# Two layers of attention and feed-forward on one core: the front of the first batch in the setup, stacks from two queues, gates broadcast by halves, expert weights loaded one per batch

## The chip, the core and the metric

The kernel runs on one core of one Trainium2 chip. The engines are TensorE (PE, with its weight loads PEld), VectorE (DVE), ScalarE (ACT), GpSimd (POOL) and SyncE (SP), which here only issues transfers; in the kernel before it issues all of them. The metric is the device time of one execution in microseconds.

## The reference, cut to what matters

x is 8 batches of 512 tokens by 128 channels. Each of two layers has an attention part and a feed-forward part, both modulated by a conditioning vector per batch:

```python
mod = (_silu(L0_c) @ L0_wmod).reshape(L0_c.shape[0], 6, 1, -1)
sa, ca, ga, sb, cb, gb = (mod[:, 0], mod[:, 1], mod[:, 2], mod[:, 3], mod[:, 4], mod[:, 5])
ga = (2 * (ga >= 0) - 1) * jnp.maximum(jnp.abs(ga), 0.25)
gb = (2 * (gb >= 0) - 1) * jnp.maximum(jnp.abs(gb), 0.25)
h = _layernorm(x, axis=-1) * (1 + ca) + sa
x = x + ga * _L0_attn_ref(h, ...)      # 16 heads of 8, causal
h = _layernorm(x, axis=-1) * (1 + cb) + sb
x = x + gb * _L0_ffn_ref(h, ...)       # 8 experts of 176, two per token, and a shared one
# layer 1: the same frame; attention with ALiBi slopes and no mask, then a spiking feed-forward
```

```python
scores = jnp.einsum('bhqk,bhsk->bhqs', q, k) / jnp.sqrt(jnp.float32(dk))
scores = jnp.where(causal_mask, jnp.float32(-1000000000.0), scores)
weights = jax.nn.softmax(scores, axis=-1)
ctx = jnp.einsum('bhqs,bhsk->bhqk', weights, v)
return concat @ Wo + bo
```

## The kernel before

The program has five parts, one after the other: the setup, the attention of layer 0, its experts, the attention of layer 1, its spiking feed-forward. Each part is a block in which every engine has its own instruction list; a block ends when all engines are through their lists. The change is in the setup and in the first batches of the attention of layer 0.

**Setup** (`setup_phase`, from L107). SP issues the loads: cT, x of batch 0, wmod (the modulation weights, 768 KB), columns (projection weights and biases), rows, then x of batches 1 to 7 (1.75 MB), and the constant rows of the stacks. TensorE makes the gates of both layers (`setup_ps<-wmod,c_silu`, L171), eight modulations (`setup_ps<-c_silu,wmod`, L178), and the output bias. VectorE makes the layer norm statistics of batch 0, the SiLU, the gates, mods (shift and scale per channel) and scales the q weights. GpSimd clears tiles and normalises batch 0 (xn).

**The front of a batch** (helpers `front_*`, L299 to L405). VectorE makes the statistics, GpSimd 1/std and xn, TensorE transposes xn (L337), ScalarE reads it with shift and scale into hT (L355), TensorE projects q, k (L349) and v (L346), ScalarE reads q and k twice (bf16 in L363, f32 in L364) and v into VP (L369). q and k in f32 are split into three bf16 parts each by `front_split` (L374): subtract, round, subtract. SP stacks the parts into QP and KP with six transfers each (`front_stack`, L391). A matmul over such a stack gives the score of f32 q and k.

**The attention** (`attention_phase`, L408). Heads are worked in groups of four, four groups a batch, 32 groups G in all. Time goes by beats, six beats a group, 24 a batch in layer 0, and every engine's list is written by one loop over the beats from -11 to the end. Beat 0 is that of group 0's first key score. Max scores run 11 beats ahead (`max_score`, L569 and L580): queries on the partitions, VectorE reduces them (L829, L833), GpSimd makes the negative maximum in two bf16 parts (`shifts`, L915 to L918), TensorE transposes it (`max_T`, L550), ScalarE copies it (at_nrow, L742), and SP sends it with two transfers into two rows of QP (`send_rows`, L1007). Then come the key scores (`key_score`, L606), ScalarE's exponentials (L757), GpSimd's clearing above the diagonal (L946), and the values (`values`, L654) into Ob, which ScalarE copies once a group (Oev, L785). Max scores use two double banks of PSUM, key scores and fronts share three banks in turn.

SP's list is in order: a transfer waits behind all that are written before it. Per batch b it has the Q stack of b + 1, rows of group 4b + 1, the K stack of b + 1, the denominators and results of batch b - 1 gathered (den, ctxN, L241), rows of 4b + 2, the reciprocals spread through DRAM (rdram, denB, L257), rows of 4b + 3 and 4b + 4. The context of batch b - 1 is multiplied by denB on VectorE (L268), projected by TensorE with weights that GpSimd has multiplied by the gate (`finish_weights`), and added to x.

Fronts of batch n are written into batch n - 2's beats: ln at 14, q at 17, k at 20, and v at 6 of batch n - 1. For batch 1 that is beats -10, -7 and -4. Batch 0's front stands ahead of the beats.

Of the kernel before, what the change touches and what calls it, by code (L numbers as in the profile page):

```python
# [13 lines left out]
F32 = mybir.dt.float32  # L14
# [7 lines left out]
P = 128  # L22
# [83 lines left out]
def setup_phase(nc, dram, sb):  # L106

    x, ident = sb["x"], sb["ident"]
    with ExitStack() as ctx:
# [12 lines left out]
        s = semaphores(nc, ctx, "su", "c x0 bop wmod load zero ident tanh sil mm chain")  # L122
# [5 lines left out]
        def _(sp):  # L128
# [4 lines left out]
            sp.dma_start(sb["columns"][:], dram["columns"]).then_inc(s["load"], 16)  # L133
            sp.dma_start(sb["rows"][:], dram["rows"].partition_broadcast(P)).then_inc(s["load"], 16)
            sp.dma_start(x[:, SEQ:].rearrange("p (m d) -> p m d", d=D),
                         dram["x"][1:].rearrange("b (t p) d -> p (b t) d", p=P)).then_inc(sb["x_rest"], 16)
# [3 lines left out]
            sp.wait_ge(s["load"], 32)  # L140
            sp.wait_ge(s["chain"], 5)
            sp.dma_start(sb["gates_dram"], sb["gate_rows"][:]).then_inc(sb["gates_sent"], 16)

        @block.gpsimd
        def _(g):
            g.memset(ident[:], 0.0).then_inc(s["zero"], 1)
            g.memset(sb["mhalf"][:], -0.5)
            g.memset(sb["ones"][:], 1.0)
            g.memset(sb["VP"][:], 0.0).then_inc(s["zero"], 1)
# [3 lines left out]
            g.wait_ge(s["zero"], 2)  # L153
            g.memset(sb["VP"][:, :, :, :, DENS:DENS + 1], 1.0)
            front_powers(g, sb, front, 0)
            front_normalise(g, sb, front, 0)

        @block.scalar
# [5 lines left out]
        def _(t):  # L164
            t.wait_ge(s["sil"], 1)
            t.wait_ge(s["wmod"], 16)

# [7 lines left out]
            for layer in range(2):  # L175
                for i, ch in enumerate((CH_SA, CH_CA, CH_SB, CH_CB)):
                    k = layer * 4 + i
                    last = t.matmul(ps[:, 1, k * NBATCH:(k + 1) * NBATCH], wmod[:, layer, ch * D:(ch + 1) * D],  # L178
                                    sil[:, layer, :], start=True, stop=True)
            last.then_inc(s["mm"], 1)  # L180
            t.wait_ge(s["load"], 32)
# [11 lines left out]
        def _(v):  # L193
            v.wait_ge(s["x0"], 16)
            front_stats(v, sb, front, 0)
# [211 lines left out]
def attention_phase(nc, dram, sb, layer):  # L407
# [5 lines left out]
    with ExitStack() as ctx:  # L413
# [64 lines left out]
        def fills(beat):  # L478
# [5 lines left out]
            for name, when, lead in (("ln", LN_AT, 2), ("q", Q_AT, 2), ("k", K_AT, 2), ("v", V_AT, 1)):  # L484
                if at == when and 1 <= n + lead <= last_b:
                    out.append((name, n + lead))
# [1422 lines left out]
```

## Time and profile before

| | us |
|---|---|
| median of 3 runs | 1073.48 |
| lowest and highest | 1072.3 and 1075.61 |
| profiled execution | 1077.53 |
| its span on the core | 1075.8 |
| TensorE busy | 951.1 |
| VectorE busy | 784.7 |
| ScalarE busy | 755.6 |
| GpSimd busy | 539.2 |

The span is what the profiler sees on the engines, the profiled execution's own time is a little more. A busy time is that of instructions; a matmul row gives its modelled end, so a busy TensorE is not one at its peak. A line such as L349 can be a helper's and then stands for many places; the tile names and the time say which one it is. An x2 behind an f32 matmul's row means two records for each. "SPq" rows are issues of transfers by SP, with the time that the issuing took, not the transfer.

### The profile page before, as it was taken

How to read it: one execution, taken by the hardware profiler on the slowest of the kernel's cores; microseconds unless marked ns; L12 is line 12 of the kernel's file. 1: busy time of each engine (PE TensorE's matmuls, PEld its weight loads, DVE VectorE, ACT ScalarE, POOL GpSimd, SP SyncE). 2: the span in 40 equal slices, each digit the busy share in tenths (PEclk: the TensorE clock that was granted, in tenths of full speed). 3: DMA queues.
4: the chain of work that ended last, by engine and by line, in shares of the span. 5: the costliest groups of instructions: out<-in, count | busy, mean ns of one | idle time of the engine just before them, and what ended most of it. 6: DMA issues, size and time to landing. Idle time of an engine off the chain costs nothing. (4 is left out here: it accounts for less than half of the span.)

```text
span 1075.8 us, 23037 instructions
## 1 busy us (share of the span) xinstructions
PE 951.1 (88%) x8688; PEld 519.9 (48%) x8688; DVE 784.7 (73%) x1321; ACT 755.6 (70%) x1380; POOL 539.2 (50%) x751
## 2 busy tenths in 40 slices
PE   5688898889898999999999889989899998899896
PEld 3233343334344888888888623333333333333564
DVE  2567777778793766776766589888898988896465
ACT  2367777777776666666666459888888888888663
POOL 4446655675553011101130557786867778665344
PEclk9589999999999999999999979999999999999999
DMA  6432212211301533321343320203112020200011
GB/s 187 155 127 76 57 41 78 72 42 54 84 13 53 130 108 110 91 85 49 102 109 99 93 78 19 74 12 83 31 54 62 24 73 13 82 2 25 23 30 50
DMA packets 61246, 73.91 MB, mean 69 GB/s; under 512 B 14088, under 2 KB 43400, under 8 KB 60624
## 3 DMA queue, kind: packets, MB, share of 16 engines
q1 hardware_dynamic: 61136, 72.44, 24.0%
q8 instruction: 69, 1.13, 0.5%
q14 instruction: 41, 0.34, 0.1%
HBM read 39.24 MB, written 2.77 MB: 39 GB/s over the span
## 5 line engine op out<-in xcount | busy, mean ns | idle before, releaser
L757 ACT ACTIVATE at_E<-at_Sb 128x512 f32<-128x512 f32 x832 | 446.4, 598 | 94.6 <-PE at_Sb L606 88.9
L826 DVE TENSOR_REDUCE at_mx<-at_Mb 128x2 f32<-128x1024 f32 x256 | 297.2, 1217 | 39.8 <-PE at_Mb L569 38.7
L654 PE MATMUL at_Ob<-at_E,VP 128*32 128x256 f32 (+2 forms) x2816 | 215.0, 379 | 13.0 <-ACT Oev L785 7.3
L606 PE MATMUL at_Sb<-QP,KP 64*128 64x512 bf16 (+3 forms) x1024 | 202.6, 346 | 13.4 <-ACT full_k L364 3.6
L569 PE MATMUL at_Mb<-KP,QP 62*128 62x512 bf16 (+3 forms) x1024 | 181.5, 361 | 31.1 <-DVE at_mx L826 28.2
L935 POOL TENSOR_TENSOR at_E<-at_E,at_factor 128x512 f32<-128x512 f32 x128 | 162.4, 1272 | 79.7 <-ACT at_E L757 69.7
L829 DVE TENSOR_REDUCE at_mx<-at_Mb 128x2 f32<-128x768 f32 (+1 forms) x128 | 138.2, 1087 | 72.3 <-PE at_Mb L569 71.1
L946 POOL TENSOR_SCALAR_AFFINE_SELECT at_E<-at_E 128x512 f32<-128x512 f32 x128 | 82.7, 659 | 83.2 <-ACT at_E L757 83.2
L569 PEld LDWEIGHTS at_Mb<-KP,QP 62*128 62x128 bf16 x1024 | 55.0, 97 | 125.9 <-DVE at_mx L826 73.4
L654 PEld LDWEIGHTS at_Ob<-at_E,VP 128*32 128x32 f32 x2816 | 57.0, 108 | 115.2 <-issue 86.0
L606 PEld LDWEIGHTS at_Sb<-QP,KP 64*128 64x128 bf16 x1024 | 74.8, 96 | 74.1 <-ACT at_E L757 34.9
L1355 DVE TENSOR_TENSOR ex_hh<-ex_R,ex_th 128x512 f32<-128x512 f32 x88 | 66.0, 751 | 57.9 <-ACT ex_th L1299 57.2
L1299 ACT ACTIVATE ex_th<-ex_z 128x512 f32<-128x512 f32 x88 | 55.6, 632 | 67.7 <-DVE ex_z L1345 66.4
L1345 DVE SCALAR_TENSOR_TENSOR ex_z<-ex_Ab,columns,ex_up 128x512 f32<-128x512 f32 x104 | 77.7, 748 | 30.9 <-ACT ex_up L1284 27.2
L1457 PEld LDWEIGHTS ex_Yb<-ex_w,ex_hh 128*128 128x128 f32 x704 | 91.3, 191 | 13.6 <-DVE ex_hh L1355 7.1
L1457 PE MATMUL ex_Yb<-ex_w,ex_hh 128*128 128x128 f32 x704 | 93.5, 276 | 3.7 <-DVE ex_hh L1355 3.7
L1284 ACT ACTIVATE ex_up<-ex_Bb,columns 128x512 f32<-128x512 f32 x104 | 70.9, 682 | 16.5 <-PE ex_Bb L1441 11.3
L1065 POOL TENSOR_TENSOR ex_rstd<-ex_ve,mhalf 128x4 f32<-128x4 f32 x8 | 8.2, 1020 | 146.9 <-DVE ex_ve L1059 146.9
L833 DVE TENSOR_REDUCE at_mx<-at_Mb 128x4 f32<-128x1024 f32 x64 | 59.9, 953 | 5.1 <-PE at_Mb L569 4.3
L654 PE MATMUL at_Ob<-at_E,at_VD 128*32 128x128 f32 (+1 forms) x1024 | 60.5, 332 | 0.0
L1439 PE MATMUL ex_Ab<-ex_h_hi,ex_w_hi 128*128 128x512 f32 x104 | 50.2, 483 | 2.4 <-PEq L413 1.3
L785 ACT ACTIVATE Oev<-at_Ob 128x512 f32<-128x512 f32 x64 | 38.9, 607 | 5.9 <-PE at_Ob L654 5.9
(185 smaller groups left out, 1428.3 us busy)
## 6 DMA issues: line engine op xcount, KB each, us to landing
QP<-q SPq DMA_DIRECT2D x96, 128.0 KB, 2.4
KP<-k SPq DMA_DIRECT2D x96, 128.0 KB, 2.4
ex_R<-rw_dram SPq DMA_DIRECT2D x32, 256.0 KB, 4.2
ctxN<-Oev SPq DMA_DIRECT2D x16, 256.0 KB, 2.9
denB<-rdram SPq DMA_DIRECT2D x64, 64.0 KB
ex_R<-rw_dram SPq DMA_DIRECT2D x16, 224.0 KB, 4.5
ex_R<-rw_dram SPq DMA_DIRECT2D x16, 192.0 KB, 3.6
ex_R<-rw_dram SPq DMA_DIRECT2D x16, 160.0 KB, 3.4
```

Source lines behind the costliest of these rows:

```text
L569: return pe.matmul(out[:, c, at:at + width], QP[p0:p0 + ROWS_M, b % 2, hp, qt * P:(qt + 1) * P], KP[p0:p0 + ROWS_M, b % 2, hp, 0:width], s ...
L606: return pe.matmul(out[:, at:at + SEQ - q0], KP[p0:p0 + ROWS_H, b % 2, 2 * g + a, kt * P:(kt + 1) * P], QP[p0:p0 + ROWS_H, b % 2, 2 * g + ...
L654: last = pe.matmul(Ob[VW * i:VW * (i + 1), 0, q0:q1], weights_of(b, G, kt, i, q0), moving, start=(kt == 0 and q0 == 0), stop=False, skip_g ...
L757: nc.scalar.activation(dst, src, ACT.Exp).then_inc(s["s_read"], 1)
L826: v.tensor_reduce(mx[:, G % 2, :, t % 2, t // 2], src, AX.X, ALU.max).then_inc(s["m_read"], 1)
L829: v.tensor_reduce(mx[:, G % 2, :, t % 2, qt], src[:, :, 0:(qt + 1) * P], AX.X, ALU.max)\
L935: p.tensor_tensor(blocks, blocks, factor[:, GROUP * g:GROUP * (g + 1), :], ALU.mult)\
L946: last = p.affine_select(out=blocks, in_=blocks, compare_op=ALU.is_ge, fill=0.0, base=0, pattern=[[0, GROUP], [1, P]], channel_multiplier=-1)
L1284: nc.scalar.activation(up3[:, q, :], Bb[:, q, :], ACT.Identity, bias=b3[:, j:j + 1]).then_inc(s["u3"], 1)
L1345: v.scalar_tensor_tensor(z[:, q, :], Ab[:, q, :], b1[:, j:j + 1], up3[:, q, :], ALU.add, ALU.mult).then_inc(s["z"], 1)
L1355: v.tensor_tensor(hh[:, r % 2, :], R[:, r % RING, :], th[:, r % 2, :], ALU.mult)\
L1457: last = pe.matmul(Yb[:, 0, t * P:(t + 1) * P], hidden[:, t * P:(t + 1) * P], w2[:, j, :], start=(j == 0 and t == 0), stop=(j == N - 1), s ...
```

## The change

In the setup, the SiLU goes ahead of the statistics. The two modulations that layer 0's attention needs come first, then the gates, then the whole front of batch 0: transposes, hT, q, k, v, in four PSUM banks of its own (`setup_front`). GpSimd splits q, VectorE splits k. SP issues Q's stack and ScalarE K's, both within the setup. The other six modulations and the output bias come behind. x of batch 1 is loaded on its own.

In the attention of layer 0, the front of batch 0 is gone from the lists, the front of batch 1 moves from beats -10, -7 and -4 to -2, 1 and 4, and its statistics from ahead of the beats to behind beat -8's reduction. x of batches 2 to 7 is loaded behind group 0's rows. The gates (`gates`, broadcast from DRAM to 128 partitions, 2 MB) come in two halves of 1 MB: layer 0's in batch 0 behind group 2's rows, layer 1's in batch 2 behind group 10's rows. Of w1, w3 and w2 (832 KB each) one is loaded in each of batches 1, 2 and 3. The lists of layer 1 keep their order; it only waits for its half of the gates.

```diff
 setup, SP
-            sp.dma_start(x[:, SEQ:].rearrange("p (m d) -> p m d", d=D),
-                         dram["x"][1:].rearrange("b (t p) d -> p (b t) d", p=P)).then_inc(sb["x_rest"], 16)
             front_rows(sp, dram, sb, 0, 0, front["const"])
             for name in ("maskq", "maskk"):
                 sp.dma_start(sb[name][:], dram[name]).then_inc(front["const"], 16)
+            sp.dma_start(x[:, SEQ:2 * SEQ].rearrange("p (t d) -> p t d", t=TILES),
+                         dram["x"][1].rearrange("(t p) d -> p t d", p=P)).then_inc(sb["x1"], 16)
+            sp.dma_start(sb["rows"][:], dram["rows"].partition_broadcast(P)).then_inc(s["load"], 16)
+            front_stack(sp, sb, front, 0, 0, 2)
 setup, GpSimd
+            g.wait_ge(front["s_read"], 2)
+            front_split(g, sb, front, "q", 0)
 setup, ScalarE
+            a.wait_ge(s["mods"], 1)
+            a.wait_ge(front["s_fill"], 1)
+            front_hT(nc, sb, front, 0, 0, fb[:, 0, :])
+            a.wait_ge(s["scaled"], 1)
+            for i, which in enumerate("qk"):
+                a.wait_ge(front["s_fill"], 2 + i)
+                front_qk(nc, sb, front, 0, which, fb[:, 1 + i, :])
+            a.wait_ge(s["vp"], 1)
+            a.wait_ge(front["s_fill"], 4)
+            front_v(nc, sb, front, 0, fb[:, 3, :])
+            front_stack(a, sb, front, 1, 0, 3)
 setup, TensorE
+            modulation(0, 0)
+            modulation(0, 1).then_inc(s["mm"], 1)
...
+            front_transpose(t, sb, front, 0, fb[:, 0, :])
+            t.wait_ge(s["scaled"], 1)
+            t.wait_ge(front["s_read"], 1)
+            for i, which in enumerate("qkv"):
+                front_project(t, sb, front, 0, which, fb[:, 1 + i, :])
+            for layer, i in ((0, 2), (0, 3), (1, 0), (1, 1), (1, 2), (1, 3)):
+                last = modulation(layer, i)
 setup, VectorE
+            v.tensor_tensor(full[:], full[:], parts["k0"][:], ALU.subtract).then_inc(front["r"], 1)
+            v.wait_ge(front["r"], 2)
+            v.wait_ge(front["p1"], 1)
+            v.tensor_copy(parts["k1"][:], full[:]).then_inc(front["p1"], 1)
+            v.wait_ge(front["p1"], 2)
+            v.wait_ge(front["p2"], 1)
+            v.tensor_tensor(parts["k2"][:], full[:], parts["k1"][:], ALU.subtract).then_inc(front["p2"], 1)
 attention, beats
+        EARLY = {-2: "ln", 1: "q", 4: "k"} if causal else {}
 attention, VectorE
+                if causal and beat == -8:
+                    v.wait_ge(sb["x1"], 16)
+                    front_stats(v, sb, s, 1)
+                    front_aggregate(v, sb, s, 1)
 attention, GpSimd
+                if causal and beat == -7:
+                    front_powers(p, sb, s, 1)
+                    normalise(1)
+                if causal and beat in EARLY and beat > 0:
+                    split(EARLY[beat], 1)
 attention, SP
-                stack(0, 0)
-                stack(0, 1)
-                sp.wait_ge(sb["gates_sent"], 16)
-                sp.dma_start(sb["gates"][:], sb["gates_dram"].partition_broadcast(P)).then_inc(sb["gates_ready"], 16)
+            send_rows(0)
+                sp.dma_start(sb["x"][:, 2 * SEQ:].rearrange("p (m d) -> p m d", d=D),
+                             dram["x"][2:].rearrange("b (t p) d -> p (b t) d", p=P)).then_inc(sb["x_rest"], 16)
+                if b == 0 and causal:
+                    send_rows(1)
+                    stack(1, 0)
+                    stack(1, 1)
+                elif b < last_b:
                     stack(b + 1, 0)
+                    send_rows(GROUPS * b + 1)
                     stack(b + 1, 1)
-                if b == 0 and causal:
-                    for dst, src in ((sb["w_raw"]["w1"], "w1"), (sb["w_raw"]["w3"], "w3"), (sb["w2"], "w2")):
-                        sp.dma_start(dst[:], dram[src]).then_inc(sb["experts_loaded"], 16)
+                if 1 <= b <= 3 and causal:
+                    dst, src = ((sb["w_raw"]["w1"], "w1"), (sb["w_raw"]["w3"], "w3"), (sb["w2"], "w2"))[b - 1]
+                    sp.dma_start(dst[:], dram[src]).then_inc(sb["experts_loaded"], 16)
+                if b == 0 and causal:
+                    sp.wait_ge(sb["gates_sent"], 16)
+                    sp.dma_start(sb["gates"][:, :, 0:2 * P], ...).then_inc(sb["gates_ready"], 16)
+                if b == 2 and causal:
+                    sp.dma_start(sb["gates"][:, :, 2 * P:4 * P], ...).then_inc(sb["gates_late"], 16)
```

What this does to the lists is seen at two places. First TensorE, from the end of the setup to the first key scores. at_Mb are max scores, at_Sb from `ident,xn` the transposes of batch 1, from `hT,columns` its q or k, from `idb,at_nmx` the transposed maximum, from `QP,KP` key scores. Before:

```order
L337 MATMUL at_Sb<-ident,xn 128x128 x4
...
L569 MATMUL at_Mb<-KP,QP 128x256 x4
L349 MATMUL at_Sb<-hT,columns 128x512
L589 MATMUL at_Mb<-maskk,maskq 128x256 x2
...
L550 MATMUL at_Sb<-idb,at_nmx 32x128
L349 MATMUL at_Sb<-hT,columns 128x512
L580 MATMUL at_Mb<-maskk,maskq 128x128 x2
...
L606 MATMUL at_Sb<-QP,KP 128x512 x2
```

And now:

```order
L605 MATMUL at_Sb<-idb,at_nmx 32x128
L635 MATMUL at_Mb<-maskk,maskq 128x128 x2
...
L387 MATMUL at_Sb<-ident,xn 128x128 x4
L644 MATMUL at_Mb<-maskk,maskq 128x2x128 x2
...
L661 MATMUL at_Sb<-QP,KP 128x512 x2
L399 MATMUL at_Sb<-hT,columns 128x512
L635 MATMUL at_Mb<-maskk,maskq 128x128 x2
...
L661 MATMUL at_Sb<-QP,KP 128x256 x2
L399 MATMUL at_Sb<-hT,columns 128x512
```

Batch 1's transposes now stand behind the transposed maximum of group 0, and its two projections behind key scores of beats 1 and 4. Second SP, from the first stack on. Before:

```order
L403 DMA QP<-q 16x8x512 x6
L403 DMA KP<-k 16x8x512 x6
...
L1019 DMA gates<-gates_dram 128x4096
L1007 DMA QP<-at_nrow 2x8x128 x2
L403 DMA QP<-q 16x8x512 x6
L1007 DMA QP<-at_nrow 2x8x128 x2
L403 DMA KP<-k 16x8x512 x6
L1031 DMA w_raw<-in_w 128x1664 x2
L1031 DMA ex_w<-in_w 128x1664
L1007 DMA QP<-at_nrow 2x8x128 x6
```

And now, from the first row transfers on:

```order
L1055 DMA QP<-at_nrow 2x8x128 x2
L1065 DMA x<-in_x 128x24x128
L1055 DMA QP<-at_nrow 2x8x128 x2
L453 DMA QP<-q 16x8x512 x6
L453 DMA KP<-k 16x8x512 x6
L1055 DMA QP<-at_nrow 2x8x128 x2
L1091 DMA gates<-gates_dram 128x8x256
L1055 DMA QP<-at_nrow 2x8x128 x4
L453 DMA QP<-q 16x8x512 x6
L1055 DMA QP<-at_nrow 2x8x128 x2
L453 DMA KP<-k 16x8x512 x6
L1082 DMA w_raw<-in_w 128x1664
```

The three weight matrices no longer stand together ahead of group 2's rows; x of batches 2 to 7 stands ahead of group 1's rows, half of the gates ahead of group 3's, and the first weight matrix behind the K stack of batch 2.

## Rows read from the trace of the kernel before

**Rows 1.** page section 1, busy time, share of the span and instructions:
```profile
PE 951.1 (88%) x8688; PEld 519.9 (48%) x8688; DVE 784.7 (73%) x1321; ACT 755.6 (70%) x1380; POOL 539.2 (50%) x751
```

**Rows 2.** windows: stretch, length, busy (x instructions) per engine, PEclk, DMA share, GB/s:
```profile
30.00:40.00 10.00, 8.06 (x42) 2.82 (x42) 6.82 (x7) 2.04 (x3) 1.18 (x3) 0.50 0.74 271
...
60.00:70.00 10.00, 6.28 (x58) 2.05 (x62) 5.29 (x12) 4.31 (x10) 5.09 (x11) 0.73 0.58 238
```

**Rows 3.** timeline, setup: start, us, engine, line, op, out<-in, [idle before, releaser]:
```profile
6.55 1.87 PE L171 MATMUL setup_ps<-wmod,c_silu 128*8 128x128 f32 x8 [6.55 <-DMA wmod<-in_wmod]
...
6.94 1.74 POOL L328 TENSOR_SCALAR xn<-x,nmean,rstd 128x128 f32<-128x128 f32 x4
...
8.35 3.58 PE L178 MATMUL setup_ps<-c_silu,wmod 128*128 128x8 f32 x16
...
14.86 0.42 DVE L232 COPY bopB<-setup_ps 128x256 f32<-128x256 f32 x1 [1.31 <-PE setup_ps L188]
...
16.01 1.08 PE L337 MATMUL at_Sb<-ident,xn 128*128 128x128 f32 x4 [1.19 <-PEq L109]
...
21.37 3.83 SPq L403 DMA_DIRECT2D QP<-q  x6
...
23.49 1.07 ACT L369 ACTIVATE VP<-at_Sb 128x512 f32<-128x512 f32 x1 [0.44 <-PE at_Sb L346]
...
25.25 3.85 SPq L403 DMA_DIRECT2D KP<-k  x6
...
31.05 0.29 PE L580 MATMUL at_Mb<-maskk,maskq 64*128 64x128 bf16 x2 [7.60 <-DMA KP<-k]
```

**Rows 4.** timeline, statistics of one batch and the beats before the first exponential:
```profile
4.16 0.87 DVE L303 BATCH_NORM_STATS2 st<-x 128x6 f32<-128x128 f32 x4 [4.16 <-DMA x<-in_x]
...
5.80 1.02 POOL L321 TENSOR_TENSOR rstd<-ve,mhalf 128x4 f32<-128x4 f32 x1 [0.60 <-DVE ve L315]
...
31.80 4.09 DVE L829 TENSOR_REDUCE at_mx<-at_Mb 128x2 f32<-128x1024 f32 x4 [13.81 <-PE at_Mb L569]
...
35.84 2.07 PE L349 MATMUL at_Sb<-hT,columns 128*128 128x512 f32 x2
...
43.18 0.27 PE L550 MATMUL at_Sb<-idb,at_nmx 128*32 128x128 bf16 x1 [3.22 <-POOL at_nmx L918]
...
48.32 0.63 PE L606 MATMUL at_Sb<-QP,KP 64*128 64x512 bf16 x2
```

**Rows 5.** timeline, the row transfers of groups 1 and 2:
```profile
52.59 1.15 SPq L1007 DMA_DIRECT2D QP<-at_nrow  x2
...
54.86 0.10 PEld L606 LDWEIGHTS at_Sb<-QP,KP 64*128 64x128 bf16 x2 [0.17 <-DMA QP<-at_nrow]
...
57.64 1.09 SPq L1031 DMA_DIRECT2D w_raw<-in_w  x2
...
60.17 23.98 SPq L1007 DMA_DIRECT2D QP<-at_nrow  x6
...
66.84 0.61 PE L606 MATMUL at_Sb<-QP,KP 64*128 64x512 bf16 x2 [3.28 <-DMA QP<-at_nrow]
```

**Rows 6.** timeline, ScalarE's reading of each group's result, groups 0, 1, 4, 5:
```profile
61.09 0.60 ACT L785 ACTIVATE Oev<-at_Ob 128x512 f32<-128x512 f32 x1
...
74.86 0.61 ACT L785 ACTIVATE Oev<-at_Ob 128x512 f32<-128x512 f32 x1
...
102.56 0.60 ACT L785 ACTIVATE Oev<-at_Ob 128x512 f32<-128x512 f32 x1
...
110.86 0.61 ACT L785 ACTIVATE Oev<-at_Ob 128x512 f32<-128x512 f32 x1
```

**Rows 7.** timeline, one projection; rows of group 6 and their first reader:
```profile
76.18 1.12 PE L349 MATMUL at_Sb<-hT,columns 128*128 128x512 f32 x2
...
101.64 1.19 SPq L1007 DMA_DIRECT2D QP<-at_nrow  x2
...
104.91 0.38 PE L606 MATMUL at_Sb<-QP,KP 64*128 64x512 bf16 x2
```

More of the change, by code:

```diff
@@ L173, in _ @@
             last.then_inc(s["mm"], 1)
[L175 to L179, printed above, removed]
+            t.wait_ge(s["ident"], 1)
+            front_transpose(t, sb, front, 0, fb[:, 0, :])
[5 more added lines that the diff above has]
+                last = modulation(layer, i)
             last.then_inc(s["mm"], 1)
-            t.wait_ge(s["load"], 32)
             for layer in range(2):
@@ L193, in _, with modulated, scale @@
         def _(v):
-            v.wait_ge(s["x0"], 16)
-            front_stats(v, sb, front, 0)
-            front_aggregate(v, sb, front, 0)
+            def modulated(layer, i):
+                k = layer * 4 + i
+                return v.tensor_scalar(sb["mods"][:, layer, i, :], ps[:, 1, k * NBATCH:(k + 1) * NBATCH],
+                                       float(i % 2), None, ALU.add)
+            def scale(layer):
+                for name, width in (("wqkv", D), ("bqk", 1)):
+                    w = sb[f"{name}{layer}"][:, 0:width]
+                    last = v.tensor_scalar(w, w, float(DK) ** -0.5, None, ALU.mult)
+                return last
             v.wait_ge(s["tanh"], 1)
@@ L201, in _ @@
             v.tensor_scalar(sil[:], sil2[:], 0.5, None, ALU.mult).then_inc(s["sil"], 1)
+            v.wait_ge(s["x0"], 16)
+            front_stats(v, sb, front, 0)
+            front_aggregate(v, sb, front, 0)
             v.wait_ge(s["mm"], 1)
+            modulated(0, 0)
+            modulated(0, 1).then_inc(s["mods"], 1)
+            v.wait_ge(s["columns"], 16)
+            scale(0).then_inc(s["scaled"], 1)
+            v.wait_ge(s["mm"], 2)
             src = ps[0:NBATCH, 0, :]
@@ L483, in fills @@
             n, at = divmod(beat, BPB)
+            if beat in EARLY:
+                out.append((EARLY[beat], 1))
             for name, when, lead in (("ln", LN_AT, 2), ("q", Q_AT, 2), ("k", K_AT, 2), ("v", V_AT, 1)):
-                if at == when and 1 <= n + lead <= last_b:
+                if at == when and (FIRST if lead == 2 else 1) <= n + lead <= last_b:
                     out.append((name, n + lead))
@@ L1739, in build @@
                 sb[n] = sb[whole][:, parts[n]:parts[after]]
[L1740 removed]
+        for n in ("x1", "x_rest", "gates_late", "gates_sent", "gates_ready", "stored", "apart"):
             sb[n] = ctx.enter_context(nc.semaphore(n))
```

90 lines of the change are left out of this document (39 added, 51 removed).

## The prediction

> **What bounds the kernel now.** I read the page first: TensorE is busy for 88% of the span and no other engine for more than 73% [rows 1]. That is an average over stages. The change touches the start and the first batches, so the windows of ten microseconds come next: in 30 to 40 the granted clock is 0.50, half of the 2.4 GHz level, and in 60 to 70 it is 0.73 with TensorE busy for 6.28 of 10 us [rows 2]. These are the two places where time can be had, and the timeline says why.
>
> At the start TensorE waits 7.60 us for the K stack: the twelve stack transfers leave one queue, Q's six from 21.37 and K's six from 25.25, 3.85 us for six, and the first max score starts at 31.05 [rows 3]. From there to the first key score at 48.32 it is 17.27 us, for 11 beats. In them stand both projections of batch 1, of which the first takes 2.07 us at the low clock, and a wait of 3.22 us for GpSimd, which splits batch 1's q before it makes group 0's shifts [rows 4].
>
> At 63.6 a second hole opens: group 2's row transfer is issued at 60.17, behind three weight matrices of 832 KB issued from 57.64 on, and its reader starts at 66.84 after a wait of 3.28 us [rows 5]. The price is read from ScalarE's result copies: groups 0 to 1 lie 13.77 us apart, the undisturbed groups 4 to 5 lie 8.30 apart, so the hole and the slow clock behind it cost 5.5 us [rows 6].
>
> **Part 1, front of batch 0 in the setup.** The SiLU goes ahead of the statistics on VectorE, which moves nothing: TensorE's first matmul waits for wmod until 6.55 either way. Then come two modulations (3.58 us for eight, 0.45 each: 0.9) and the four gate matmuls (1.87), until 9.3. xn is ready at 8.68, so the four transposes start at 9.3 where they started at 16.01 [rows 3]: 6.7 us earlier. What follows up to the reading of v is the same chain on the same engines, so v is read by 24.56 - 6.7 = 17.9, Q's stack is issued from 14.7 to 18.5, and K's, now on ScalarE's queue behind that reading, from 17.9 to 21.7. Before, K's data was usable 1.95 us after the last issue (29.10 to 31.05), so now at 23.7. The setup itself must also end: v's matmuls end at about 16.8, six modulations add 2.7, and from there to the next block is what lay between 11.93 and 16.01, 4.1 us: 23.6 [rows 3]. I take 23.8 for the first max score, 7.2 earlier. SP's issues of constants no longer stand behind 1.75 MB of x, so I see nothing of them on this path.
>
> No row shows ScalarE issuing a transfer. The nearest row is SP's, 0.64 us each; at twice that K's stack would come 3.8 us later, at nothing it would still wait for its third part and for the end of the setup. So 0 to 3.8 us against, and I take 0.
>
> VectorE makes k's parts instead of GpSimd. Its three operations lie within the time in which ScalarE issues K's first three transfers (1.9 us from 17.9), and k is read before v, so by 16.8 (23.49 - 6.7). I count it at nothing; on GpSimd it would have stood behind q's parts.
>
> What the second queue is worth is small: on SP alone K's issues would start at 18.5 and not at 17.9, so 0.6 us. The Trainium skill speaks against more (DMA: Bandwidth & Descriptors, Issuing engines are not separate DMA queues): queues share the same 16 DMA engines, and a second one saves only the sequencer's time. By that rule, the sum holds as it stands, since I count no faster transfer; whoever counts on two parallel streams would put 3.8 us more into it.
>
> **Part 2, the beats before the first key score.** The statistics of batch 1 now stand on VectorE after four reductions: 4.09 us for four, and 1.64 us from the statistics' start to GpSimd's power (4.16 to 5.80) [rows 4]. So: 23.8 + 0.75 until VectorE starts + 4.09 + 1.64 = 30.3; power and normalisation end 2.88 us later (5.80 to 8.68) [rows 3, 4] at 33.2; group 0's shifts are queued behind them on GpSimd, and with the transpose and the copy on ScalarE I give them 1.6 us, to 34.8. A row transfer needs 2.3 us from issue to reader (52.59 to 54.86) [rows 5]: 37.1. By VectorE alone: ten reductions at 1.02 and the statistics give 36.4, and 0.7 of TensorE: the same 37.1. I take 37.2 for the first key score against 48.32: 11.1 us earlier. TensorE no longer stops for long between 9.3 and there, so I expect the full clock in it; VectorE sets the pace, and I count nothing for it.
>
> **Part 3, q and k of batch 1 in beats 1 and 4.** They are no longer in the beats before. Now they stand among key scores: 1.12 us each at full clock [rows 7], 2.24, with ScalarE's four readings ahead of exponentials. Ends: 0, where TensorE waits for VectorE anyway, and 4.1, both at the low clock [rows 4]. I take 2.5.
>
> **Part 4, weights spread, gates halved, x last.** The hole in batch 0 goes: 5.5 us. What is late next are the other transfers ahead of row transfers. A row transfer has 3.3 us from issue to need (101.64 to 104.91) [rows 7] and uses 2.3, so its slack is 1.0 us. Ahead of one there now are 1.5 MB of x (group 1's rows, issued about five us later), one weight matrix in each of batches 1 to 3, before the gathering of the denominators, which VectorE waits for in order, and half of the gates in batches 0 and 2, the latter before the denominators' way through DRAM. The 2.5 MB took from 57.64 to about 65 [rows 5], so 0.34 MB a microsecond: 832 KB need 2.5 us, of which all but the last part passes before the rows of group 6 are issued 3 us later. Low end 0. High end: each is wholly in front of its reader, 4.4 + 2.9 + 3 x 2.5 + 2.9 less 1.0 of slack each, some 12 us. I take 2.5: 0.5 for each matrix and 1 for the late gates, near the low end, because the queue's issues keep them apart.
>
> **The sum.** 11.1 - 2.5 + 5.5 - 2.5 = 11.6 us. The profiled execution took 1077.53 us (span 1075.8), so 1065.9; it lies 4 us above the median 1073.48, and on the median's scale the forecast is 1062.
>
> **Rivals.**
> (a) The end of the setup moves by less: ScalarE's issues are slow, or the constants come late. For it speaks that TensorE's order in the setup is now one chain through four engines; against it, that each step has a row. Price 3 to 5 us: 1066.
> (b) Batch 1 comes late. Its k is read in beat 4, split by GpSimd behind three diagonal operations, and stacked on SP; A beat is 1.4 us (8.30 / 6) [rows 6]: k is projected by 5 x 1.4 + 1.1 = 8.1 after the first key score, reading and split with their queues are some 5, the last issues and the landing 3, so 16; TensorE asks for it in beat 13, at 13 x 1.4 + 2.5 = 20.7. A margin of 4 to 5, estimated from these rows. If the splits slip a group, TensorE waits 4 us with a lower clock behind it: 1066 to 1068.
> (c) Each large transfer stops its reader for about its whole length, but the clock holds: 12 in place of 2.5, gain 2: 1071.
> (d) Slower than before: the same waits, each drawn out as the one in the trace was, where 3.28 us of waiting cost 5.5, a factor of 1.7, since the clock fell behind it [rows 2, 5, 6]. The place is the key score that opens groups 1, 6, 10, 14 and the context of batch 1. 12 x 1.7 = 20 in place of 2.5: 1062 + 17.5 = 1079. It decides from 8.3 us of pure waiting on. Against it: the weights were three in a row, and no two large transfers now stand together.
> (e) More is gained: the projections of part 3 hide, and no new wait shows: 5 us more, 1057.
>
> **How the numbers follow.** Forecast, 1058 to 1066: 0.60. (a) 0.10 and (b) 0.08, both faster; (c) 0.08, of which 0.05 within 0.3%; (d) 0.05, of which 0.01 within; (e) 0.09. 0.3% is 3.2 us, about what a measurement of this kernel can tell from no change. Faster 0.60 + 0.10 + 0.08 + 0.03 + 0.09 = 0.90, same 0.06, slower 0.04. The range 1055.5 to 1069 leaves out (c), (d) and a little of (e).
>
> **What would show it.** In the profile after: transposes at about 9.3, K's six issues on ScalarE's queue from about 17.9, the first max score at about 23.8 with a granted clock of 1.00 before and behind it, the first key score at 37.2, groups 0 and 1 read about 8.7 us apart, q and k of batch 1 between key scores at 1.12 us. Wrong would be: a wait of TensorE for a row transfer in groups 1, 6, 10 or 14, of VectorE for den or denB in batches 1 to 3, or of TensorE for the stacks at beat 13, of more than 1 us each. The forecast falls if the first key score stands later than 41, or if batches 1 to 3 together take over 5 us longer than before.

## The result and the profile after

The changed kernel took 1065.92 us (median of 5 runs, 1064.44 to 1066.16), the kernel before 1075.61 beside it (5 runs, 1072.3 to 1078.66): a ratio of 0.9908 [0.9881, 0.9935], 9.7 us less. Run again with the experiments it gave 0.9906 [0.9872, 0.994] and 0.9934 [0.9914, 0.9955]. The profiled execution took 1066.16 us, its span is 1064.4 where it was 1075.8.

Section 1 of the page after, engines busy in us, answers to [rows 1]: the work is the same, the span is shorter.

```profile
PE 945.7 (89%) x8688; PEld 517.6 (49%) x8688; DVE 788.3 (74%) x1324; ACT 754.2 (71%) x1380; POOL 537.5 (50%) x748
```

Two windows of it, with the columns of [rows 2]:

```profile
30.00:40.00 10.00, 6.18 (x43) 2.51 (x45) 9.20 (x19) 0.78 (x2) 3.32 (x8) 0.50 0.01 3
...
60.00:70.00 10.00, 9.14 (x103) 3.68 (x99) 6.71 (x8) 8.21 (x17) 5.75 (x12) 1.00 0.09 29
```

In 30 to 40 the granted clock is still 0.50, against the forecast, but VectorE is busy for 9.20 of 10 us where it had 6.82: it sets the pace there. In 60 to 70 TensorE works for 9.14 us at the full clock (1.00); the hole is gone.

The timeline of the front, answering to [rows 3] and [rows 4]:

```profile
8.88 0.99 PE L184 MATMUL setup_ps<-c_silu,wmod 128*128 128x8 f32 x4 [8.88 <-DMA wmod<-in_wmod]
...
11.61 1.12 PE L387 MATMUL setup_front<-ident,xn 128*128 128x128 f32 x4
...
17.19 4.04 SPq L453 DMA_DIRECT2D QP<-q  x6
...
18.84 4.09 ACTq L453 DMA_DIRECT2D KP<-k  x6
...
23.30 0.42 DVE L282 COPY bopB<-setup_ps 128x256 f32<-128x256 f32 x1 [0.80 <-PE setup_ps L214]
...
27.05 0.29 PE L635 MATMUL at_Mb<-maskk,maskq 64*128 64x128 bf16 x2 [3.79 <-DMA KP<-k]
...
37.17 0.27 PE L605 MATMUL at_Sb<-idb,at_nmx 128*32 128x128 bf16 x1 [1.32 <-POOL at_nmx L966]
...
40.43 0.63 PE L661 MATMUL at_Sb<-QP,KP 64*128 64x512 bf16 x2
...
42.23 1.13 PE L399 MATMUL at_Sb<-hT,columns 128*128 128x512 f32 x2
...
46.29 1.13 PE L399 MATMUL at_Sb<-hT,columns 128*128 128x512 f32 x2
```

Here wmod landed at 8.88, where it landed at 6.55 before, and everything behind it is late by as much. The last two rows are q and k of batch 1, now among key scores. The same kernel profiled again (a0 below) had wmod at 6.21, and is the better copy to compare:

```profile
6.21 1.00 PE L184 MATMUL setup_ps<-c_silu,wmod 128*128 128x8 f32 x4 [6.21 <-DMA wmod<-in_wmod]
...
9.01 1.09 PE L387 MATMUL setup_front<-ident,xn 128*128 128x128 f32 x4
...
14.56 4.03 SPq L453 DMA_DIRECT2D QP<-q  x6
...
16.21 4.01 ACTq L453 DMA_DIRECT2D KP<-k  x6
...
24.01 0.29 PE L635 MATMUL at_Mb<-maskk,maskq 64*128 64x128 bf16 x2 [2.87 <-DMA KP<-k]
```

A table by stage says where the time went. Its borders are starts of rows: the first max score, the first key score, and ScalarE's result copies (Oev, line 836, [rows 6]) of groups 0, 1, 14, 31 (end of layer 0's attention), 32 (the first of layer 1's attention, with layer 0's experts ahead of it) and 63 (its last). All in us, one profiled execution each.

| stage | before | after | a0 | a1 | e1 | e2 | e9 | e8 |
|---|---|---|---|---|---|---|---|---|
| to first max score | 31.05 | 27.05 | 24.01 | 23.96 | 24.37 | 24.77 | 24.18 | 22.57 |
| to first key score | 17.27 | 13.38 | 13.35 | 13.36 | 13.36 | 13.36 | 13.37 | 13.37 |
| to group 0 | 12.77 | 15.43 | 15.64 | 15.72 | 16.72 | 15.39 | 15.65 | 15.50 |
| groups 0 to 1 | 13.77 | 8.17 | 8.15 | 8.16 | 16.28 | 8.16 | 8.15 | 8.18 |
| groups 1 to 14 | 121.55 | 126.07 | 126.62 | 124.00 | 121.94 | 122.73 | 124.55 | 122.82 |
| groups 14 to 31 | 145.37 | 145.45 | 145.39 | 145.37 | 145.36 | 145.37 | 144.67 | 145.48 |
| groups 31 to 32 | 308.50 | 308.73 | 308.81 | 310.05 | 308.72 | 308.73 | 308.55 | 308.87 |
| groups 32 to 63 | 352.01 | 346.64 | 348.89 | 350.55 | 349.08 | 350.75 | 345.22 | 345.28 |

a0 and a1 are the changed kernel again, the e's are experiments. Down to group 14 the change is worth 6.3 us in the first profile, 8.6 in a0 and 11.2 in a1. The row below that one no edit of the change touches, and it hardly moves. The last row holds layer 1's attention, which the change leaves as it is but for waiting for its half of the gates, and yet three profiles of one kernel lie 3.9 us apart in it; e9 is about that.

What is new between groups 1 and 14 stands in ScalarE's rows of the profile after, beside the queue's:

```profile
87.91 0.60 SPq L1082 DMA_DIRECT2D w_raw<-in_w  x1
88.56 0.61 SPq L291 DMA_DIRECT2D den<-Oev  x1
89.21 0.58 SPq L292 DMA_DIRECT2D ctxN<-Oev  x1
...
94.31 0.60 ACT L836 ACTIVATE Oev<-at_Ob 128x512 f32<-128x512 f32 x1 [1.33 <-DMA ctxN<-Oev]
...
132.42 0.60 ACT L836 ACTIVATE Oev<-at_Ob 128x512 f32<-128x512 f32 x1 [2.89 <-DMA ctxN<-Oev]
...
171.47 0.60 ACT L836 ACTIVATE Oev<-at_Ob 128x512 f32<-128x512 f32 x1 [1.14 <-DMA ctxN<-Oev]
```

The copy of groups 4, 8 and 12 overwrites Oev, which the gathering of the batch before (ctxN) must first have read, and that gathering is issued 1.3 us behind a weight matrix. Before, these copies waited for no transfer [rows 6]. The waits view of the stretch 80 to 325 (what waited, for whom: us in total, times, longest) sums it and shows VectorE's, which I had priced instead:

```profile
ACT Oev L836 <- DMA ctxN<-Oev: 5.4, 3, 2.9
...
DVE rden L299 <- DMA den<-Oev: 1.4, 1, 1.4
```

### The profile page after: what moved, and what is told of

The parts are those of the page before. It is cut to its first block and busy times, and to the rows that moved or that the text cites. A ratio compares the mean times of both kernels' runs of the same rounds, so it can differ in the third digit from the quotient of the medians.

```text
span 1064.4 us, 23048 instructions
## 1 busy us (share of the span) xinstructions
PE 945.7 (89%) x8688; PEld 517.6 (49%) x8688; DVE 788.3 (74%) x1324; ACT 754.2 (71%) x1380; POOL 537.5 (50%) x748
## 3 DMA queue, kind: packets, MB, share of 16 engines
q8 instruction: 69, 1.13, 0.4%
## 5 line engine op out<-in xcount | busy, mean ns | idle before, releaser
L709 PE MATMUL at_Ob<-at_E,VP 128*32 128x256 f32 (+2 forms) x2816 | 213.8, 377 | 16.5 <-ACT Oev L836 10.2
L624 PE MATMUL at_Mb<-KP,QP 62*128 62x512 bf16 (+3 forms) x1024 | 181.5, 360 | 23.6 <-DVE at_mx L872 20.3
L1342 ACT ACTIVATE ex_up<-ex_Bb,columns 128x512 f32<-128x512 f32 x104 | 70.9, 682 | 16.6 <-PE ex_Bb L1499 11.6
L836 ACT ACTIVATE Oev<-at_Ob 128x512 f32<-128x512 f32 x64 | 38.9, 608 | 11.2 <-PE at_Ob L709 5.9
```

The lines of the kernel that those rows point to most:

```text
L624: return pe.matmul(out[:, c, at:at + width], QP[p0:p0 + ROWS_M, b % 2, hp, qt * P:(qt + 1) * P], KP[p0:p0 + ROWS_M, b % 2, hp, 0:width], s ...
L709: last = pe.matmul(Ob[VW * i:VW * (i + 1), 0, q0:q1], weights_of(b, G, kt, i, q0), moving, start=(kt == 0 and q0 == 0), stop=False, skip_g ...
L1342: nc.scalar.activation(up3[:, q, :], Bb[:, q, :], ACT.Identity, bias=b3[:, j:j + 1]).then_inc(s["u3"], 1)
```

## The experiments

The theory after the result: the front gives 11, q and k of batch 1 cost little, one weight matrix per batch removes the 5.5 us hole and brings back some of it as ScalarE's waits for ctxN. The rivals: the weights never mattered; the front is set by the constants' order, by the number of queues, or by who makes k's parts. Runs of the kernel before on the same chip stand beside each.

**a0, the changed kernel again**, with 15 runs of the kernel before.

> The changed kernel itself, as the reference for the others on the same chip. The profiled one had its first max score at 27.05, its first key score at 40.43, the result of group 1 read at 64.03, of group 12 at 171.47 and of group 31 at 335.55. Theory A (the gain lies in layer 0 alone: 10.8 us by group 1, of which 4.5 are given back in batches 1 to 3; the rest of the 11.4 between the two profiled spans is layer 1 waiting for den and denB by chance): these five come within 0.3 us again and the time is 6 to 10 us below before. Rival B (layer 1 gains from the change as well, as its order of transfers differs): layer 1 again takes 5 us less than in the kernel before.

Measured: 1066.12 (1062.6 to 1069.82, 5 runs) against 1076.3 (1070.72 to 1080.31, 15 runs), 0.9906 [0.9872, 0.994]. In layer 0 its table column differs from the first profile by 3.0 us ahead of the first max score, where wmod landed 2.7 earlier, and by less than 0.6 in every row behind it. Neither theory came whole. The five runs lie 7.2 us apart, not 0.3. Layer 1's attention took 3.1 us less than in the one profile of the kernel before (A: nothing, B: 5), in a1 1.5 less, and the experiments that leave layer 1 alone range from 349.1 to 353.4 us there, around the 352.0 of before. So no gain of the change in layer 1 is shown.

**e1, the weights together again**: the three transfers back in one batch, at the same place.

```diff
-                if 1 <= b <= 3 and causal:
-                    dst, src = ((sb["w_raw"]["w1"], "w1"), ...)[b - 1]
-                    sp.dma_start(dst[:], dram[src]).then_inc(sb["experts_loaded"], 16)
+                if b == 0 and causal:
+                    for dst, src in ((sb["w_raw"]["w1"], "w1"), ...):
+                        sp.dma_start(dst[:], dram[src]).then_inc(sb["experts_loaded"], 16)
```

> The three weight matrices go back behind the K stack of batch 1, together; all else as in the changed kernel. Theory A: spreading them traded one hole for three waits (ScalarE's reading of groups 4, 8 and 12 waits for ctxN, which is queued behind a matrix). So here group 2's key score waits again some 3 us and groups 0 to 1 or 1 to 2 lie 4 to 6 us further apart, while the intervals before groups 4, 8 and 12 shrink by 2.0, 2.0 and 1.2 us: group 31 within 1 us of the changed kernel. Rival B (the prediction): the matrices cost 0.5 us each where they are now, so together they are 4 us slower.

Measured: 1071.23 (1067.43 to 1075.82, 10 runs), 0.9962 [0.9938, 0.9985], 5.1 us above a0. Its timeline, the queue's rows and the reader's:

```profile
53.34 1.10 SPq L1082 DMA_DIRECT2D w_raw<-in_w  x2
54.48 1.21 SPq L1082 DMA_DIRECT2D ex_w<-in_w  x1
55.73 1.14 SPq L1055 DMA_DIRECT2D QP<-at_nrow  x2
...
62.52 0.61 PE L661 MATMUL at_Sb<-QP,KP 64*128 64x512 bf16 x2 [5.92 <-DMA QP<-at_nrow]
```

A row transfer issued right behind three matrices reached its reader 6.8 us after its issue (55.73 to 62.52), where one alone needs 2.3 [rows 5]. Up to group 1 it takes 9.2 us longer than in a0, groups 1 to 14 are 4.7 shorter since the ctxN waits are gone; net 4.5 in layer 0, and 5.1 in the medians, with rival B's 4 nearer than theory A's 1. So spreading the weights is worth about half of the whole change, and the theory that they don't matter has fallen.

**e2, each weight matrix behind the last rows of its batch.**

```diff
+                send_rows(GROUPS * b + 3)
+                if 1 <= b <= 3 and causal:
+                    ...the same three lines, taken from ahead of the gathering
```

> Each matrix is issued behind the rows of the batch's fourth group, where SP then has nothing to issue for some 10 us, and no longer ahead of den and ctxN. Theory A: no wait of ScalarE for ctxN is left, groups 4, 8 and 12 are read 7.7 to 8 us behind their predecessors, group 31 comes 4.5 to 5.2 us earlier (330.8). Rival B: the waits for ctxN are not due to the matrix, and group 31 moves by less than 1.5.

Measured: no copy of Oev waits for ctxN in layer 0, and groups 1 to 14 take 122.73 (a0 126.62, a1 124.00). The median is 1065.06 (1064.35 to 1066.4, 4 runs), 1.1 below a0's, which is less than the runs differ by. The queue's and ScalarE's rows of e2, the same gathering and copy as above:

```profile
85.54 0.61 SPq L291 DMA_DIRECT2D den<-Oev  x1
86.19 0.58 SPq L292 DMA_DIRECT2D ctxN<-Oev  x1
...
90.59 0.60 ACT L836 ACTIVATE Oev<-at_Ob 128x512 f32<-128x512 f32 x1
```

So the mechanism is shown by the trace: with the matrix out of the way, the copy starts with no wait. Its price is 1.3 to 3.9 us in groups 1 to 14 (against a1 and a0), less than the 4.5 to 5.2 of theory A; by the medians alone it would not be shown. 1.2 us over before remain between groups 1 and 14, all of it between groups 1 and 4; which edit they belong to was not tried.

**e3, the constants issued once wmod has landed**: SP waits for wmod ahead of the spare rows and masks.

```diff
+            sp.wait_ge(s["wmod"], 16)
             front_rows(sp, dram, sb, 0, 0, front["const"])
```

> SP waits for wmod to land before it issues the constant rows, masks, x of batch 1 and rows. Theory A: wmod landed at 8.88 and not at 6.55 because four transfers of constants share the engines with it; without them TensorE starts at about 6.6, and the chain up to the stacks moves 2.2 us ahead: first max score at 25, group 31 2 us earlier. Rival B: the constants then come as late as the stacks, or wmod is late for another reason: first max score at 27 or later.

Measured: the first wmod matmul at 6.35 and the first max score at 24.47, as in a0 (6.21, 24.01); 1068.49 (1064.54 to 1070.32, 5 runs), 0.9922 [0.9891, 0.9952]. The edit shows nothing by itself, since the lateness did not come again without it either. But small transfers alone do not hold wmod back: in nine of ten further profiles of kernels that issue them as the changed one does, wmod was usable at 6.2 to 6.4, in one at 6.8 (e2), without any wait. The 8.88 of the first profile came in that one alone. What made it late is open.

**e4, the second half of the spare rows behind send_rows(0).**

```diff
-            if causal:
-                front_rows(sp, dram, sb, layer, 1, s["const2"])
...
+                front_rows(sp, dram, sb, layer, 1, s["const2"])
```

> The four transfers of constant rows for the second half of the stacks are issued behind group 0's rows and not at the start of the attention. In the changed kernel's second run SP issued Q's first part at 14.56, ScalarE issued K's last one by 20.22, and the first max score came at 24.01, 3.8 us later, with the transfer engines full. Theory A: the stacks are bound by the transfer engines, and these four (512 KB) run beside K's last parts: without them K lands 0.5 to 1.5 us earlier, 8 to 9 us behind Q's first issue. Rival B: the lag belongs to the second queue or to the end of the setup; 9.4 us as before.

Measured in one run: first max score at 23.91 with wmod at 6.20, first key score at 37.26, 1068.12 us. No effect, and the run could have had none: in a0 SP issues these four from 21.87 on, and from 22 to 23 ScalarE's queue (q10), with K's parts, is the only one that moves bytes.

```profile
q10 hardware_dynamic: 214, 0.19, 99.9%
```

So they never ran beside the stacks, and e4 does not test whether the transfer engines limit these.

**e5, both stacks on SP's queue.**

```diff
             front_stack(sp, sb, front, 0, 0, 2)
+            front_stack(sp, sb, front, 1, 0, 3)
...
-            front_stack(a, sb, front, 1, 0, 3)
```

> K's stack is issued by SP behind Q's, in the setup, and by no other queue. Theory A (bound by the transfer engines): the two stacks take 9.5 to 9.9 us from Q's first issue to the first max score, as on one queue in the kernel before (21.37 to 31.05, 9.68), against 9.45 with two; the second queue is worth less than 0.5 us. Rival B: the second queue hides K's issues, 3.8 us; then the first max score comes 2 us or more later than with two.

Measured in one run: 1068.8 us. Its timeline:

```profile
14.55 4.04 SPq L453 DMA_DIRECT2D QP<-q  x6
...
18.63 3.83 SPq L453 DMA_DIRECT2D KP<-k  x6
...
24.40 0.29 PE L635 MATMUL at_Mb<-maskk,maskq 64*128 64x128 bf16 x2 [3.27 <-DMA KP<-k]
```

On one queue K's last issue ends at 22.46 and the data is there 1.94 us later; on two it ends at 20.22 and the data comes 3.79 later (a0). From Q's first issue to the first max score it takes 9.85 us on one queue, and 8.94 to 9.86 with a mean of 9.54 in ten profiles with two. The windows of a0 (columns as in [rows 2]) show both queues at work:

```profile
18.00:20.00 2.00, 0.08 (x1) 0.08 (x1) 1.83 (x10) 0.00 (x0) 0.03 (x1) 0.68 1.10 233
20.00:22.00 2.00, 1.14 (x4) 0.84 (x4) 0.42 (x1) 0.00 (x0) 0.00 (x0) 0.50 1.15 226
```

They move 233 and 226 GB/s at a DMA share of 1.10 and 1.15 (packets laid over one another give more than 1), where e5 with one queue moves 184 and 201 at 0.66 and 0.74. So a second queue does move about a fifth more while both run, but each packet takes longer. That the transfer engines are full is likely from this and not shown: from 22 to 23, with ScalarE's queue alone, the share is 1.00 at 191 GB/s, no more bytes than e5's queue moves at 0.74. The second queue is worth 0.3 us by the mean, and at most 0.9. The Trainium skill says (DMA: Bandwidth & Descriptors, Issuing engines are not separate DMA queues) that transfers of all issuers run on the same engines, and that a second issuer saves only the issuing time. The trace agrees that there is no more to be had, and shows less: 2.24 us of issuing were saved in a0, and 1.85 of them came back as a longer landing.

**e6, k's parts made by GpSimd behind q's.**

```diff
             front_split(g, sb, front, "q", 0)
+            g.wait_ge(front["s_read"], 3)
+            front_split(g, sb, front, "k", 0)
```

and VectorE's three operations removed.

> GpSimd makes k's parts behind q's, VectorE none. With two queues and VectorE, k's last part is ready at 19.0, 4.5 us behind Q's first issue. Theory A: GpSimd needs 1.15 + 0.62 + 1.15 us for each, so k's last part is ready 5.8 to 6 us behind Q's first issue, still ahead of the transfers in front of it; the first max score moves by less than 0.5 us. Rival B: K's last transfer waits for it, and the first max score comes 1.3 us later.

Measured in one run: 9.17 us from Q's first issue to the first max score, inside the 8.94 to 9.86 above; 1067.11 us. GpSimd ends k's parts at 20.00, and ScalarE's queue ends K's issues at 20.65 (14.94 + 5.71, where a0's take 4.01), so the parts do hold the queue a little, but the first max score does not come later by it. The edit that gives k's parts to VectorE is worth nothing that a run shows.

**e7, the front of batch 1 ahead of the first key score too**: its statistics ahead of the beats, layer norm, q and k at beats -10, -7 and -4 in place of -2, 1 and 4, the splits behind them, and the Q stack ahead of send_rows(1).

```diff
-        EARLY = {-2: "ln", 1: "q", 4: "k"} if causal else {}
+        EARLY = {-10: "ln", -7: "q", -4: "k"} if causal else {}
...
-                    send_rows(1)
                     stack(1, 0)
+                    send_rows(1)
                     stack(1, 1)
```

> The front of batch 0 stays in the setup, but that of batch 1 goes back to beats -10, -7 and -4, with its statistics ahead of the beats and the stacks in the old order. The changed kernel: 13.35 us from the first max score to the first key score, and 23.8 from there to the reading of group 1's result. Theory A: moving it into beats -2, 1 and 4 saved some 3.8 us before the first key score and cost 2.5 behind it, so here 17 us and then 21 to 21.5, and group 1's result is read 1 to 1.5 us later than in the changed kernel. Rival B: the late front costs as much as it saves, or batch 1's stack is late in it: group 1 or 4 is then read at the same time or earlier here.

Measured: 1073.27 (1069.8 to 1077.12, 10 runs) against 1074.85 (13 runs), 0.9997 [0.9978, 1.0016]: no gain over the kernel before can be told any more. Group 1's result is read at 67.59, 6.4 us later than in a0, where 1 to 1.5 was expected. The timeline of e7:

```profile
37.35 2.04 PE L399 MATMUL at_Sb<-hT,columns 128*128 128x512 f32 x2
...
40.35 6.94 SPq L453 DMA_DIRECT2D QP<-q  x6
...
47.33 1.13 SPq L1055 DMA_DIRECT2D QP<-at_nrow  x2
...
51.68 0.39 PE L661 MATMUL at_Sb<-QP,KP 64*128 64x512 bf16 x2 [2.89 <-DMA QP<-at_nrow]
```

The first key score is at 42.26, 4.9 later than in a0: the projections and a second normalisation lie on VectorE's, GpSimd's and TensorE's way there, at the low clock (2.04 us for one projection, against 1.13). And the Q stack's issues take 6.94 us behind 1.5 MB of x, where six took 4.03, so that group 1's rows leave only at 47.33 and their reader waits 2.89. So of the 11.0 us that the front gained, 4.9 belong to moving batch 1's front, and 6.1 to batch 0's front in the setup. The edit moves three things at once (statistics, projections, stack order); what each costs was not tried.

**a1, the changed kernel a third time**, beside e8 and e9.

> The changed kernel once more, as the reference on this chip. All theories: first key score at about 37.4 where wmod lands at 6.2 to 6.8 us, group 31 at 333 to 336, and 0.990 of the time of the kernel before.

Measured: 1067.04 (1066.33 to 1069.19, 5 runs) against 1076.09 (1071.65 to 1076.57, 10 runs), 0.9934 [0.9914, 0.9955].

**e9, layer 1's reciprocal one beat later**, the changed kernel otherwise. This is outside the change: the profiles of before, after, a0 and a1 all show VectorE waiting for den in layer 1.

```diff
-            (14, 17, 20, 6, 9, 17, 19) if causal else (24, 26, 28, 8, 10, 20, 22))
+            (14, 17, 20, 6, 9, 17, 19) if causal else (24, 26, 28, 8, 11, 20, 22))
```

> The changed kernel with one edit: in layer 1 the reciprocal of the denominators stands in beat 11 and not in 10 on VectorE. Theory A: the spread between executions (1062.6 to 1069.8 for the changed kernel, 1070.7 to 1080.3 for the one before) comes from VectorE's waits for den in layer 1; here they are gone, groups 32 to 63 take 345 to 346 us (346.6 to 352.0 so far), the median is 3 us lower and the spread smaller. Rival B: den's wait only moves to the reading of ctxN or to denB: same time and same spread.

Measured: 1060.91 (1059.46 to 1062.79, 5 runs), 0.9876 [0.9855, 0.9897], 6.1 us below a1 on the same chip. The waits view of layer 1 (336 to 1010, with the last batch's wait for denB in both) in a1:

```profile
DVE ctxT L318 <- DMA denB<-rdram: 6.8, 3, 5.1
...
DVE rden L299 <- DMA den<-Oev: 4.2, 6, 1.4
```

and in e9:

```profile
DVE ctxT L318 <- DMA denB<-rdram: 7.5, 3, 5.1
...
DVE rden L299 <- DMA den<-Oev: 0.8, 1, 0.8
```

The reciprocal's waits are almost gone, and they did not move to denB, which is rival B: the last batch waits 5.07 us for it here and 5.09 in a1. Groups 32 to 63 take 345.2 us, as theory A expected (345 to 346), 5.3 less than in a1; the rest of the profiles' difference, 1.5, lies in groups 31 to 32, ahead of the edit. The profiles bear the theory out: VectorE's waits for den in layer 1 add up to 2.4 us in the profile after, 3.3 in a0, 4.2 in a1 and 6.6 before, and groups 32 to 63 take 346.6, 348.9, 350.6 and 352.0; with 0.8 in e9 and e8 it is 345.2 and 345.3. So the differences in this stage between executions of one kernel go with these waits, though not one for one: against a1 3.4 us of waits are gone and 5.3 gained, against the profile after 1.6 and 1.4; how was not traced. Twice the expected 3 us came by the medians. That the spread gets smaller is not shown: the five runs lie 3.3 us apart, a1's 2.9.

**e8, three edits put together**: e2's weights, the late half of the gates behind the rows of group 19 (batch 4), and e9's reciprocal.

> The changed kernel with the three matrices and the late half of the gates issued behind the rows of a batch's fourth group (batches 1 to 3, and 4), and in layer 1 the reciprocal in beat 11 in place of 10. Theory A: no wait for ctxN, and the one for denB in batch 2 (3.8 us) goes too, so group 31 is read at 328.5 to 329.5, 4.5 us ahead of the changed kernel; layer 1 loses its waits for den, 2.5 to 5.0 us in the runs so far, of which I count 3. Together 7 us below the changed kernel, about 1058. Rival B: the waits in layer 1 are made up by the reductions that stand behind them and the later reciprocal delays denB in the last batch: 4 us below and no more.

Measured: 1058.84 (1057.18 to 1060.09, 5 runs), 0.9852 [0.983, 0.9874]: the fastest kernel of this study, 8.2 us below a1 and 17.3 below the kernel before beside it. Against e9 it is 2.1 less by the medians, with runs that just overlap. In the two profiles groups 1 to 14 are 1.7 shorter (122.82 against 124.55), as e2 promised, and the first max score comes 1.6 earlier for another reason (see the clock, below). The wait for denB in layer 0, which I expected to go with the late gates, is still there, 3.7 us.

## Why the forecast was right, and where its steps were off

The forecast was 1062 by the median and 11.6 us less on the profiled execution. Measured were 1065.92, 3.9 more and inside the range, and medians that differ by 9.7, 10.2 and 9.1 us. Of the 3.9, 2.1 are the base, since the median of the kernel before came out at 1075.61 and not at 1073.48, and 1.8 are a smaller gain. The profiled executions differ by 11.4, which looks like a hit and is partly chance: 6.2 of it lies in layer 0's attention and 5.1 behind it, where the change is not shown to do anything. In the forecast's own terms a0 gives 11.0 - 2.9 + 5.6 - 5.1 = 8.6 down to group 14, and a1 gives 11.0 - 2.9 + 5.6 - 2.4, or 11.2 before rounding, for the 11.1 - 2.5 + 5.5 - 2.5 = 11.6 of the sum: three terms were right, and one was mis-sized.

**Front (11.1 forecast).** Right in size: 31.05 + 17.27 = 48.32 before, 37.36 in a0, so 11.0 (the first profile, with wmod late, has 40.43 and gives 7.9). The first max score came at 24.01 for 23.8, and the beats from there took 13.35 for 13.4. Two steps inside it were wrong and cancelled. ScalarE's queue began K's issues at 16.21 and not at 17.9, since it does not wait for the end of the reading of v (16.14 to 17.25), only for its start; and K's data came 3.79 us behind the last issue and not 1.95, since the packets of both queues ran beside one another and took longer (e5, and a0's windows). Both stacks together take 9.5 us from Q's first issue with either number of queues. The 0 to 3.8 us that I had set against ScalarE's issuing were rightly taken as 0: its six took 4.01, SP's 4.03.

**Clock.** I expected 1.00 up to the first key score, which my own sum spoke against: it left TensorE idle from 19.5 to 23.8. In a0 the granted clock is 0.68 in 18 to 20 and 0.50 in 20 to 22; TensorE was busy for 0.08 us of the first of these windows and then waited 2.87 us for K's stack. The window 30 to 40 of the profile after shows that it stays at 0.50 through the beats. There it cost nothing, as the 13.35 shows: VectorE's reductions, busy for 9.20 of 10 us in the window above, set the pace. The step failed and no term of the sum hung on it.

In the setup there was a pace to be gained that I did not see. The projections of q and k, in a0 and in e8, whose setup is the same:

```profile
11.12 3.75 PE L399 MATMUL setup_front<-hT,columns 128*128 128x512 f32 x4 [1.02 <-ACT hT L405]
...
11.14 1.96 PE L399 MATMUL setup_front<-hT,columns 128*128 128x512 f32 x4 [1.03 <-ACT hT L405]
```

They took 1.96 us in e6 and e8 and 3.5 to 3.8 in the ten other profiles that make the front in the setup, and 3.78 in the kernel before, whose chain I had taken over. Where they are fast Q's first issue comes at 13.63 (e8) and 13.78 (e6) for 14.56 in a0, and the first max score at 22.57 and 22.95 for 24.01. A factor of two is what lies between a projection at 0.50 and at 1.00 (2.04 and 1.13 us), but the windows show 1.00 in this stretch in both, so what makes the difference is open.

**q and k of batch 1 (2.5), the hole (5.5).** The copy of group 0 lies between the two. Up to it the changed kernel takes 2.7 to 2.9 us more than the kernel before (12.77 against 15.43, 15.64 and 15.72), the price of q and k there (each of the two projections takes 1.13 us, as forecast); from there to group 1 it takes 8.2 for 13.77, so the hole was worth 5.6. e1 puts the weights back in front of a row transfer and loses 9.2 us. The transfer itself takes no longer there than in the kernel before (6.8 us from issue to reader, and 60.17 to 66.84, so 6.7); its reader waits longer for it, 5.92 us for 3.28.

**New waits (2.5).** This is the mis-sized term, in amount and in kind. (The rows that I named for the 2.5 MB landing at about 65 do not show it; the windows of the kernel before do, roughly: 414 GB/s in 63 to 65, 277 in 65 to 66, 39 in 66 to 67.) Measured over groups 1 to 14 against before: 4.5 (after), 5.1 (a0), 2.4 (a1). Of it 1.2 remain in e2, so one matrix in front of the gathering costs 1.3 to 3.9 over three batches, 0.4 to 1.3 each for my 0.5. I gave it to VectorE's wait for den; the trace shows 1.4 us of that, once, and 5.4 us of ScalarE's copies waiting for ctxN, the second gathering behind the same matrix, whose reader's buffer I had not followed. The late gates, priced at 1, show no wait at all: the one wait of VectorE for denB in layer 0, 3.7 to 3.9 us, stands in the last batch, in all of before, after, a0 and e2, and e8, which moves the gates away, has it too. Two of the signs of being wrong were touched: VectorE's one wait for den was over 1 us, and batches 1 to 3 (from the copy of group 3 to that of group 15) took 4.0, 5.1 and 2.5 us longer than before in after, a0 and a1, where over 5 was to bring the forecast down.

**Rivals.** (a) did not come: in a0 the setup's last copy ends at 21.60, ahead of the 23.6 that I had for its end. What came once was a late wmod, which made 3.0 us in the first profile; how many of the executions without a profile had it is not known. (b) did not come: no wait of TensorE for stacks at beat 13. (c) and (d) rested on large transfers stopping their readers for their length; spread out they don't (e2 is 1 us from a0), placed right in front of rows they make the reader wait (5.92 us in e1). (e) asked for no new wait; e2 shows that this would have been worth 1.3 to 3.9 us in layer 0.

The mis-sized term is 0 to 2.6 us too small, which covers the 1.8 by which the medians gained less; but the medians of the kernel before alone lie at 1074.85 to 1076.3 in the four series, so a difference of this size is not firmly told from noise.

## What to carry to other kernels

Before putting a bulk transfer on a queue, list the small transfers issued behind it until it has landed, and for each the readers of its target and the writers that reuse its source; a copy that must not overwrite what a gathering still reads is such a waiter too, and it is on another engine than the gathering's reader. A second issuing queue saves issuing time, and here most of that came back as later landing, so price it by the time from first issue to first use and not by the issues. And compare stages of several profiles before crediting a difference to a change: in a stage that it doesn't touch one kernel moved by 3.9 us from run to run. When two waits are compared, take windows that end at the same work, not at the same time.

## What the runs showed of the hardware

A transfer of the same 768 KB (wmod), issued at the same time, was usable at 6.2 to 6.8 us in all thirteen profiles but one, where it was 8.88, and the whole front moved with it.

Small gatherings behind an 832 KB matrix in one queue are late by an amount that changes from run to run: ScalarE's copies waited 1.33, 2.89 and 1.14 us in the profile after, 1.77, 1.77 and 2.43 in a0, 0.97, 1.56 and 1.15 in a1.

ScalarE's queue begins to issue transfers while an ACTIVATE that stands ahead of them in its list still runs: in a0 the reading of v runs from 16.14 to 17.25, K's issues start at 16.21.

A small VectorE operation took eleven times as long beside a GpSimd memset. The timeline of the profile after:

```profile
1.64 3.50 POOL L154 MEMSET VP<- 128x4096 f32 x1
2.68 0.17 DVE L235 SCALAR_TENSOR_TENSOR c_silu<-c_tanh,cT 128x16 f32<-128x16 f32 x1 [2.68 <-ACT c_tanh L165]
2.89 2.29 DVE L237 TENSOR_SCALAR c_silu<-c_silu 128x16 f32<-128x16 f32 x1
```

The TENSOR_SCALAR ends at 5.18, with the memset (5.14); the SCALAR_TENSOR_TENSOR just ahead, beside the same memset, took 0.17, and in the kernel before, behind the memset, the same TENSOR_SCALAR took 0.20. The Trainium skill has a rule that fits (SBUF — State Buffer, Who interferes with whom): a VectorE copy or tensor_scalar may take the port pair that it shares with GpSimd, and whoever comes second is blocked for the whole instruction. The trace agrees in what it shows, the blocking until the memset's end; which port path the instruction took, no run shows. It cost nothing here, since wmod landed later, at 6.20 at the earliest.
